# Where the scale of a layer norm, an output tile and the output products stand in four interleaved turns

## The reference

```python
x = x + xattn(layernorm(x), ctx, ctx, mask, ...)      # 16 heads of 32, 64 features each
#   q, k, v = heads(x Wq), heads(ctx Wk), heads(ctx Wv)
#   q', k' = relu(q Wqf), relu(k Wkf) * mask
#   kv, k_sum = sum over keys of k' v, of k'
#   out = (q' kv) / (q' k_sum + 1e-8);  out @ Wo.T + bo
x = x + ffn(layernorm(x), w_gate, w_up, w_down, g)
#   activation_quant: 127 / max|x| of the row, rounded;  weight_quant: sign-like, by mean|w|
#   activated = up * relu(gate)^2;  subln(activated) * g;  quantised again, times w_down
```

## Time and profile before

| | |
|---|---|
| runs, us | 410.38, 409.49, 407.21 |
| profiled execution, us | 408.24 |
| its span, us | 406.5 |
| TensorE matmuls busy, us | 382.3 (94%) |
| VectorE busy, us | 343.1 (84%) |
| ScalarE busy, us | 315.5 (78%) |
| GpSimd busy, us | 244.3 (60%) |
| granted TensorE clock, mean | 0.992 |

### The profile page before, as it was taken

One profiled execution on the slowest core, in us unless ns is written; L12 is line 12 of the kernel. 1 busy time (PEld: TensorE's weight loads), 2 busy tenths in 40 slices (PEclk: granted clock), 3 DMA queues, 4 the chain that ended last, 5 costly groups with the idle time before them and its releaser, 6 DMA issues.

```text
span 406.5 us, 8234 instructions
## 1 busy us (share of the span) xinstructions
PE 382.3 (94%) x2886; PEld 187.1 (46%) x2886; DVE 343.1 (84%) x709; ACT 315.5 (78%) x446; POOL 244.3 (60%) x223
## 2 busy tenths in 40 slices
PE   2995999999999799999999999999999999999986
PEld 1443545554545365454645444343444443444432
DVE  3759597697989999889878979999999989897983
ACT  5485477697968798995987778796979795989880
POOL 1064828998036784538445856576777756778660
PEclk9997999999999999999999999999999999999999
DMA  7766974980367640775930423132535352444365
GB/s 253 230 203 153 379 279 114 225 181 2 83 179 217 122 129 2 157 224 101 246 131 2 81 53 65 38 75 50 112 70 113 70 115 61 92 90 97 74 130 156
DMA packets 90905, 52.39 MB, mean 129 GB/s; under 512 B 78832, under 2 KB 78832, under 8 KB 90736
## 3 DMA queue, kind: packets, MB, share of 16 engines
q1 hardware_dynamic: 90864, 51.87, 49.8%
HBM read 28.78 MB, written 4.19 MB: 81 GB/s over the span
## 4 chain that ended last, share of the span: by engine, by line
PE 49%; DVE 27%; issue 6%; ACT 5%; POOL 5%; SPq 4%; DMA 2%; DVEq 1%; ACTq 0%; POOLq 0%
PE ps L1363 32%; PE ps L1428 10%; DVE amax L1238 4%; PE ps L1445 3%; POOL fl L862 2%; PE ps L1395 2%; DVE fh L1233 2%; DVE w L1233 2%; PE ps L1411 2%; DVE xq L1593 2%; DVE o L1174 2%; DVE var L1258 1%; DVE top L1249 1%; POOL o L756 1%; DVE o L1281 1%
## 5 line engine op out<-in xcount | busy, mean ns | idle before, releaser
L1428 PE MATMUL ps<-tern,area 128*128 128x512 bf16 x512 | 114.5, 379 | 2.5 <-DVE w L1233 2.3
L1428 PEld LDWEIGHTS ps<-tern,area 128*128 128x128 bf16 x512 | 49.2, 98 | 63.7 <-DVE w L1233 3.8
L862 POOL TENSOR_TENSOR v<-w 128x512 f32<-128x512 f32 x32 | 40.4, 1274 | 30.4 <-DVE w L1233 30.3
L862 POOL TENSOR_TENSOR fl<-fh,w 128x512 f32<-128x512 f32 x32 | 40.5, 1281 | 16.7 <-DVE fh L1233 16.5
L1363 PE MATMUL ps<-ctxh,w 128*128 128x512 f16 x128 | 41.5, 392 | 7.2 <-DVE ctxl L1077 7.2
L993 ACT ACTIVATE w<-ps 128x512 f32<-128x512 f32 x64 | 37.3, 582 | 12.7 <-PE ps L1428 12.7
L1363 PE MATMUL ps<-xT,w 128*128 128x512 f16 x192 | 45.2, 391 | 0.8 <-DMA xT<-o 0.8
L1363 PE MATMUL ps<-w,oT 128*128 128x512 f16 x192 | 44.0, 379 | 1.0 <-DVE o L1174 1.0
L1089 DVE SCALAR_TENSOR_TENSOR fl<-ps,fh 128x512 f16<-128x512 f32 x64 | 40.4, 680 | 4.9 <-ACT fh L900 4.7
L900 ACT ACTIVATE fh<-ps 128x512 f16<-128x512 f32 x64 | 34.1, 599 | 10.2 <-PE ps L1411 4.9
L997 ACT ACTIVATE qkT<-w 128x512 f32<-128x512 f32 x64 | 40.3, 630 | 2.0
(11 more groups left out here) (164 smaller groups left out, 896.9 us busy)
## 6 DMA issues: line engine op xcount, KB each, us to landing
tern<-in_wffn SPq DMA_DIRECT2D x24, 512.0 KB, 4.9
out<-o SPq DMA_DIRECT2D x16, 256.0 KB, 3.1
area<-in_ctxT SPq DMA_DIRECT2D x3, 1024.0 KB, 5.7
xs<-in_x SPq DMA_DIRECT2D x3, 1024.0 KB, 9.9
oT<-in_wkT SPq DMA_DIRECT2D x4, 256.0 KB, 5.3
area<-in_ctxT SPq DMA_DIRECT2D x4, 256.0 KB, 5.6
fh<-in_wvT SPq DMA_DIRECT2D x4, 256.0 KB, 7.0
xs<-in_x SPq DMA_DIRECT2D x4, 256.0 KB, 8.1
```

The costliest lines, as they stand in the source:

```text
L862: nc.gpsimd.tensor_tensor(actg[s % 2][:, q], acts[s % 2][:, q], subln[:, q], ALU.mult)\
L1428: mm = nc.tensor.matmul(acc, xqT[:, s % XT, k, :], weights[k][:, 512 * c:512 * c + 512], start=(k == 0), stop=(k == KC - 1))
```

## The change

Turn one: V3 stands behind N6 and N7 and not ahead of them; "root2" moves from behind N0 to behind K2, the last "weigh" from behind V3 to behind K3, "scale2" from behind N3 to behind V1. GpSimd splits output tile (1,2) and adds the bias of tile 3 before it splits query tile (2,3), and splits (1,3) before it copies the mask columns. SyncE's queue has the transposition of (1,2) ahead of that of query tile (2,3). Turn two: "root2" moves from V1 to K0 (behind chunks 6 and 7), "scale2" from behind N2 to behind V1. Turn three: the output products P0, P1 and P2 each stand one G later; "quant2" 0 moves from behind G10 to behind G11. FFN: "cubes2" moves from behind quarter 18 to behind quarter 19.

```diff
@@ TURNS[1]
-        "R6 R7 O3 K2 V1 N0 N1 N2 N3 N4 N5 V2 K3 V3 "
-        "N6 N7 W0 "),
+        "R6 R7 O3 K2 V1 N0 N1 N2 N3 N4 N5 V2 K3 N6 "
+        "N7 V3 W0 "),
@@ TURNS[3]
-        "N0 N1 N2 N3 G1 N4 N5 G2 N6 N7 G3 P0 G4 P1 G5 "
-        "G6 P2 G7 G8 P3 G9 G10 G11 "),
+        "N0 N1 N2 N3 G1 N4 N5 G2 N6 N7 G3 G4 P0 G5 P1 "
+        "G6 G7 P2 G8 P3 G9 G10 G11 "),
@@ ACT_AFTER[1]
-        ("N", 0): (("root2",),),
+        ("K", 2): (("root2",),),
...
-        ("V", 3): (("weigh", 7),),
+        ("K", 3): (("weigh", 7),),
@@ ACT_AFTER[2]
-        ("K", 0): (("chunk", 6), ("chunk", 7)),
-        ("V", 1): (("root2",), ("norm", 3)),
+        ("K", 0): (("chunk", 6), ("chunk", 7), ("root2",)),
+        ("V", 1): (("norm", 3),),
@@ DVE_AFTER[1]
-        ("N", 3): (("scale2",),),
+        ("V", 1): (("scale2",),),
@@ DVE_AFTER[2]
-        ("N", 2): (("scale2",),),
+        ("V", 1): (("scale2",),),
@@ DVE_AFTER[3]
-        ("G", 10): (("quant2", 0),),
+        ("G", 11): (("quant2", 0),),
@@
-DVE_LATER = {14: (("quant2", 1),), 18: (("cubes2",),)}
+DVE_LATER = {14: (("quant2", 1),), 19: (("cubes2",),)}
@@ sync
             turn_o(1, 1)
+            turn_o(1, 2)
             turn_x(2, 3)
-            turn_o(1, 2)
             turn_o(1, 3)
@@ gpsimd
             add_bias(1, 2)
-            x_tile(2, 3)
             o_tile(1, 2)
             add_bias(1, 3)
+            x_tile(2, 3)
+            o_tile(1, 3)
             mask_columns(2)
-            o_tile(1, 3)
```

## The result

The changed kernel took **412.95 us** (median of five runs, 410.87 to 413.79), the kernel before, beside it, 408.22 (407.21 to 410.38). The ratio is 1.0105, 95% interval 1.0069 to 1.0141: slower by 4.3 us, between 2.8 and 5.8. The forecast had the sign and most of the places, but a loss of 1.2, and its range ended at 412.8: the loss is some three and a half times the size. The profiled execution of the changed kernel (410.87) is the fastest of its five.

A forecast was written before the change was run, and what follows sets the result against it. TensorE bounds the kernel, busy 382 of 406.5 us, with at most 6.3 us of stops to win. The terms -0.85 - 1.0 + 1.45 + 1.65 = +1.2 gave 409.4 profiled, 410.7 as median, range 405.5 to 412.8.

The forecast's parts named there:

- Turn one's end: Scale's ten instructions, run while GpSimd is idle, take 1.9 us; TensorE wins 1.7, lost again at turn two's Q0.
- Q0: Start of turn two: GpSimd's split waits for (1,0)'s landing at 134.6, delaying the query tile; Q0 starts 0.2 us early.
- rival 3: Turn two's Q0: (1,0)'s transposition lands at 136.2, so Q0 starts 1.4 us late; 412.3 us, chance 0.15.
- Turn two's end: Stops of 0.74 and 0.24 go, mask copies come 0.5 earlier; S0 of turn three gains a further 0.65 us.
- Output products: Turn three: G4 in P0's place fills the stop of 0.95 at 228.7; a gain of 1.0 us.
- Quantising: Turn three, behind G11: the pair meets GpSimd's cast and G15's up half waits; a loss of 1.45 us.
- Cubes: FFN, behind quarter 19: the cubes meet GpSimd's casts and G23's up half waits; a loss of 1.65 us.
- rival 1: Quantising and cubes: small instructions slip in before GpSimd's; 405.7 us, or 404.2 with turn one's 1.7 kept; chance 0.25.
- rival 2: Quantising and cubes: only one of the two collisions with GpSimd happens; 408.0 us, chance 0.15.

The follow-up runs named there:

- keep_turn1: keep_turns with turn two's root2 and scale2 put back behind V1 and N2; ratio 0.9925 to the kernel before.
- b_p: The kernel before with the output products alone one G later; ratio 0.9957 to the kernel before.
- keep_mask: keep_turns with GpSimd's mask copy in turn two moved ahead of the split of output tile (2,3); ratio 0.9919 to the kernel before.
- b_cubes: The kernel before with the cubes alone moved from behind quarter 18 to behind quarter 19; ratio 1.0083 to the kernel before.
- a_order: The changed kernel with GpSimd's and SyncE's order of turn one put back; ratio 1.0046 to the kernel before.
- a_quant: The changed kernel with the first quantising of turn three put back behind G10; ratio 1.0057 to the kernel before.
- b_quant: The kernel before with the first half of the quantising alone moved from behind G10 to behind G11; ratio 1.0056 to the kernel before.
- a_cubes: The changed kernel with the cubes put back behind quarter 18; ratio 1.0009 to the kernel before.
- keep_turns: The changed kernel with turn one's GpSimd and SyncE order, the quantising and the cubes all put back; ratio 0.9965 to the kernel before.
- keep_spread: keep_mask with the quantising halves moved behind quarters 18 and 26 and the cubes behind 34; ratio 0.9909 to the kernel before.
- b_order: The kernel before with GpSimd's and SyncE's order of turn one alone changed; ratio 0.9999 to the kernel before.

## Why the prediction was right or wrong

**Turn one's end: right.** The scale's ten instructions ran from 120.91 to 122.75, 1.84 us for the 1.9 of the forecast. VectorE in the changed kernel, first and last of the ten, which answer to the earlier trace rows:

```profile
120.91 0.17 DVE L1600 RECIPROCAL ln_rstd<-ln_sd 128x4 f32<-128x4 f32 x1
...
122.59 0.16 DVE L1587 SCALAR_TENSOR_TENSOR ln_qscale<-ln_qscale,ln_rstd 128x4 f32<-128x4 f32 x1
```

TensorE was 1.9 earlier by the end of the turn (forecast 1.7). keep_turn1 less b_p gives 1.3 for it in the runs.

**Q0: the mechanism right, the landing as feared, the stop mis-judged.** GpSimd in the changed kernel, which answers to the earlier trace rows:

```profile
132.56 1.04 POOL L766 TENSOR_TENSOR o<-o,zero 128x512 f16<-128x512 f32 x1 [2.54 <-DMA oT<-o]
...
136.27 1.03 POOL L754 TENSOR_TENSOR xn<-xn,zero 128x512 f16<-128x512 f32 x1
```

The split of (1,2) waited for the landing of (1,0), which took 6.0 us from its issue at 126.47; the query tile came behind it, and Q0 started 0.2 late where 0.2 early was forecast. As a sum of starts that step was nearly exact. The prediction's own sum, TensorE 1.7 early and Q0 0.2 early, holds a stop of 1.5, so its sign for rival 3 (Q0 stands still for over 1 us) contradicted it; by the landing it was not rival 3. But "TensorE arrives early and waits" isn't neutral: the 1.9 us won became a stop of 2.02, and the clock fell behind it. The forecast counted idle time as time only.

**Turn two's end: wrong.** The stops at V2 and F0 went, as forecast. The step that failed is "S0 starts with the mask copy, which moves by 0.5": the landing ahead of it took 4.9 in place of 3.3, and TensorE, early by those two stops, stood still for 1.69. Forecast -0.65, found +1.1 in the traces. keep_mask shows that the copy's place behind that wait was what held S0.

**Output products: right.** -1.1 in the traces, -1.8 (-3.0 to -0.4) alone, against -1.0.

**Quantising: right in mechanism and size, short of the clock.** VectorE in the changed kernel, then GpSimd:

```profile
257.92 2.62 DVE L1593 TENSOR_SCALAR xq<-xs,ln_means,ln_qscale 128x512 int8<-128x512 f32 x2
260.47 0.68 DVE L1233 TENSOR_TENSOR fh<-qkT,ps 128x512 f32<-128x512 f32 x1
```
```profile
256.96 1.28 POOL L862 TENSOR_TENSOR v<-w 128x512 f32<-128x512 f32 x1 [2.07 <-DVE w L1233]
258.18 2.09 POOL L846 CAST o<-fl 128x2048 bf16<-128x2048 int16 x1
```

The pair took 2.62 (forecast 2.4) and ended 0.3 behind the cast (260.54 for 260.27), and G15 stood still for 2.37. +1.7 for 1.45; alone 2.3.

**Cubes: right in mechanism; the size is 3.4 alone, not 1.65.** VectorE, then GpSimd:

```profile
281.26 1.80 DVE L1222 TENSOR_TENSOR cube<-cube,xmax 128x4 f32<-128x4 f32 x1
283.10 0.53 DVE L1223 TENSOR_SCALAR cube<-cube,k 128x4 f32<-128x4 f32 x1
```
```profile
281.15 1.89 POOL L846 CAST o<-fl 128x2048 bf16<-128x2048 int16 x1
282.99 0.61 POOL L854 CAST area<-xq 128x512 bf16<-128x512 int8 x1
```

The second cube was issued 0.1 behind the cast and ended with it; the third ended with the next cast. The Trainium skill, "SBUF — State Buffer", section "Who interferes with whom", has the engine that comes second wait; the trace agrees: the first cube, ahead of the cast, took 0.17, the second 1.80. But only one of the five came in ahead, in the changed kernel and in b_cubes alike. The forecast's rival 1, which needed them all ahead, is out. So is rival 2, though its sign (one long stop missing, at G23) is there in the profile: the cubes collided there too, with TensorE late.

**What was missing in the sum: the clock.** -0.85 - 1.0 + 1.45 + 1.65 = +1.2 had no term for it. Putting in what was found for turn two (+1.1 for -0.65) gives +3.0, and the clock's terms of 1.7, in those executions in which they come, can make the rest. On average they are less: the mean granted clock of the change's five runs is 0.9864, that of 35 runs of the kernel before, in the set of a_order, 0.9881, which makes 0.7 us as an estimate. The kernel before has halved stretches too, and the change takes away the stops at 133 to 136 us at which some of them begin (last section). Whether one comes isn't fixed by the stop's length, as the profiles of this case have it:

| stop, us | where | halved clock behind it |
|---|---|---|
| 2.88, 2.87, 2.60 | G23: b_cubes, a_quant, a_order | yes, three of three |
| 2.37 | G15: the change | yes |
| 2.37, 2.30, 2.27 | G15: a_order, b_quant, a_cubes | no, three of three |
| 2.02, 1.99 | Q0: the change, a_quant | yes |
| 1.82 | Q0: a_cubes | no |
| 1.69 to 1.80 | S0: the change, a_order, a_quant, a_cubes, keep_turns | no, five of five |

The fall itself, worked out from the granted clock of windows of 2 us, comes between 0.3 us before the end of the stop (a_order, G23) and 1.1 behind it (a_quant, Q0).

The Trainium skill, "TensorE: Matmul & The Clock Gate", Part 1, says that recent activity decides the clock; that it is halved right behind long stops here fits, and what decides between two equal ones is not settled by these runs.

**What stays open.** Why the transposition issued at 189.0 lands after 4.9 to 5.0 us with turn two's scale moved and after 3.3 without: the order of SyncE's queue around it is the same in both. The traces do show one difference. The profile's DMA queue "instruction" moves one packet of 0.02 MB near there, and at most 1.5 us behind it all queues together fall to 30 GB/s or less for about a microsecond. In the eight traces with the late landing this comes ahead of the landing, in the six with 3.2 or 3.3 behind it. The quiet windows of the changed kernel (landing at 193.9) and of keep_turn1 (same issue, landing at 192.3):

```profile
192.40:193.80 1.40, 1.40 (x49) 1.25 (x44) 0.18 (x1) 1.40 (x3) 0.00 (x0) 1.00 0.06 6
```
```profile
193.60:195.00 1.40, 1.40 (x27) 0.82 (x20) 0.16 (x2) 1.40 (x3) 1.40 (x2) 1.00 0.21 8
```

No run moved that packet alone, so this is a coincidence of fourteen traces and not a cause that is shown. Which of two equal stops halves the clock is open too.

## What to carry to other kernels

Price a wait by where TensorE arrives: time won ahead of a fixed landing becomes a stop, and a stop of about 2 us or more can cost another 1.7 in a halved clock. Small VectorE instructions on SBUF belong where GpSimd is idle, not behind the event that starts GpSimd's longest ones. And in GpSimd's order, what TensorE wants next goes ahead of an instruction that waits for a transfer: that one line (keep_mask) was worth 1.9 us, by taking back what turn two's move had lost.

## What the runs showed of the hardware

Executions of one kernel differ by their halved stretches. keep_spread ran in 402.96 to 406.33 us, and its profiled execution (403.49) had a mean clock of 1.000 and not one such stretch ahead of its last product; that of b_p (410.67, of 405.12 to 410.67) had 0.979, with the clock at half from 33.4 to 43.7 us and from 135.8 to 142.7. The latter begins among the three stops of the earlier trace rows at 133 to 136 us, which are 1.2, 0.6 and 0.7 there, behind the second and ahead of the third: two short stops close together did what one of 1.8 did not. b_order and b_quant have such a stretch too, from 135.7 to 142.6 and from 134.8 to 138.2, the profiles of before and b_cubes, with the same stops, not at all. So a single trace can hide a cost, as it did the cubes'; here it took 6 to 12 executions of each kernel to tell the larger parts apart, and the smaller ones stay within the noise.
